# One core, convolution with generated kernels: quads in two halves, strips first and kernel pairs second, with two sets of PSUM banks

## What is computed

```
r = relu(bn(ln(x) @ w_reduce))                      # 32 channels
kgen = (r @ w_span + b_span) as (b, h, w, 16, 49)    # kernels, one for each pixel and group
x = x + sum over k of kgen[..., g, k] * patch(ln(x))[..., k, g, c]
t = tokens(x)                                        # 12544 x 128
probs = softmax(ln(t) @ gate_w + gate_b); the two largest are kept
t = t + sum over the two of prob_e * (gelu(ln(t) @ W1[e] + b1[e]) @ W2[e] + b2[e])
```

## Time and profile before

| | us |
|---|---|
| median of 3 runs | 1448.48 |
| lowest and highest | 1446.62 and 1455.89 |
| the profiled execution | 1449.3 |
| its span | 1447.5 |
| TensorE busy | 960.6 (66%) |
| ScalarE busy | 553.9 (38%) |
| VectorE busy | 497.3 (34%) |
| GpSimd busy | 488.6 (34%) |
| TensorE's granted clock, mean | 0.754 of full |

### The profile page before, as it was taken

The page is one execution under the profiler, slowest core; times in us unless marked ns, Lnnn a source line. Parts: engine busy times, 40 slices in busy tenths (PEclk is TensorE's granted clock), DMA queues, the critical chain, the costliest instruction groups (busy, mean ns, idle before and its releaser), DMA issues.

```text
span 1447.5 us, 29676 instructions
## 1 busy us (share of the span) xinstructions
PE 960.6 (66%) x11249; PEld 838.2 (58%) x11249; DVE 497.3 (34%) x1612; ACT 553.9 (38%) x1198; POOL 488.6 (34%) x536
## 2 busy tenths in 40 slices
PE   2687764888197792877928878379694687726540
PEld 1576653687096680876817768268583576725440
DVE  6111230345043450344513444123442235413432
ACT  5244330666054460453614545135351333312220
POOL 3000144012604517035171351712516136254425
PEclk9586665899598785897868778679876787656785
DMA  5659613463154532545425363252631422212322
GB/s 135 138 111 270 134 46 75 90 156 79 48 144 104 117 98 68 123 105 127 99 73 128 88 143 93 75 120 59 138 91 53 100 63 68 76 49 77 96 62 63
DMA packets 184078, 144.04 MB, mean 100 GB/s; under 512 B 65110, under 2 KB 169558, under 8 KB 183488
## 3 DMA queue, kind: packets, MB, share of 16 engines
q1 hardware_dynamic: 168114, 115.03, 33.2%
q0 software_dynamic: 14336, 25.72, 6.7%
q10 hardware_dynamic: 1486, 1.38, 0.4%
HBM read 89.70 MB, written 52.36 MB: 98 GB/s over the span
## 4 chain that ended last, share of the span: by engine, by line
PE 39%; issue 21%; another core or an unknown queue 10%; SPq 7%; ACT 7%; DVE 7%; POOL 3%; DVEq 2%; DMA 1%; ACTq 1%; POOLq 0%
PE e L1182 11%; PE kg L1148 9%; PE hy L1252 5%; PE hy L1262 5%; SPq L365 3%; POOL got L583 2%; PE back L1194 2%; ACT kb L662 2%; PE misc L1215 2%; DVEq L975 2%; ACT tn L677 2%; PE hy L1243 2%; SPq L431 1%; PE misc L1207 1%
## 5 line engine op out<-in xcount | busy, mean ns | idle before, releaser
L662 ACT ACTIVATE kb<-kg 112x896 f32<-112x896 f32 x224 | 205.6, 918 | 451.4 <-PE kg L1148 363.7
L1182 PE MATMUL e<-kb,win 112*32 112x64 f32 x6272 | 241.8, 291 | 182.3 <-issue 165.2
L583 POOL DMA_INDIRECT got<-yrows,pos x224 | 215.9, 964 | 331.9 <-DMA yrows<-yo 141.0
L1148 PE MATMUL kg<-rT,wk 98*112 98x112 f32 x1792 | 270.9, 313 | 75.5 <-ACT kb L662 42.2
L1182 PEld LDWEIGHTS e<-kb,win 112*32 112x32 f32 x6272 | 185.4, 131 | 230.1 <-issue 209.5
L569 POOL DMA_INDIRECT xrows<-tn,pos x224 | 213.8, 954 | 285.0 <-DVE pos L955 151.9
L1148 PEld LDWEIGHTS kg<-rT,wk 98*112 98x112 f32 x1792 | 233.9, 206 | 102.6 <-ACT kb L662 54.3
L712 ACT ACTIVATE hT<-hy,staged 128x128 f32<-128x128 f32 x490 | 152.6, 364 | 287.1 <-PE hy L1252 181.6
L1262 PE MATMUL hy<-staged,hT 128*128 128x128 f32 x980 | 179.7, 313 | 51.1 <-issue 22.3
L825 DVE TENSOR_TENSOR conv<-e,group_mask 128x448 f32<-128x448 f32 x112 | 69.7, 622 | 387.2 <-PE e L1182 258.4
L1252 PE MATMUL hy<-xT,staged 128*128 128x128 f32 x980 | 186.5, 321 | 19.1 <-issue 11.9
(11 more groups left out here) (113 smaller groups left out, 602.3 us busy)
## 6 DMA issues: line engine op xcount, KB each, us to landing
win<-xpad SPq DMA_DIRECT2D x56, 784.0 KB
xin<-xrows SPq DMA_DIRECT2D x56, 256.0 KB
yrows<-yo SPq DMA_DIRECT2D x56, 256.0 KB
t_row<-in_x_dram SPq DMA_DIRECT2D x64, 112.0 KB
xpad<-xs SPq DMA_DIRECT2D x240, 28.0 KB
out_dram<-t_row SPq DMA_DIRECT2D x56, 112.0 KB
xs<-in_x_dram SPq DMA_DIRECT2D x48, 112.0 KB
xrows<-tn SPq DMA_DIRECT2D x4, 896.0 KB, 14.6
```

Source lines behind the costliest of these rows:

```text
L583: pool.indirect_dma_start(got[:, slot * C:(slot + 1) * C], None, yrows[n % 2], bass.IndirectOffsetOnAxis(ap=pos[n % 2][:, k * COLS + c:k * ...
L662: act.activation(kb[:, lo:lo + 8 * PATCHES].rearrange("p (h k) -> p h k", h=2), kg[0:WIN, :].rearrange("p (h k) -> p h k", h=2)[:, :, 0:4 ...
L1148: mm = pe.matmul(kg_bank[j % 2][0:WIN, i * PATCHES:(i + 1) * PATCHES], wk[:, at:at + WIN], r[:, :, :, b4 + i], start=True, stop=True, skip ...
L1182: mm = pe.matmul(to, w[:, at:at + 32], rhs, start=True, stop=True, skip_group_check=True)
```

## The change

Each quad is split in two halves: the four strips in beats 0 to 7 (with the turns between them, the last at beat 8), and all eight pairs of the next quad in beats 8 to 15, one each. The visits move from even beats to odd ones, so that beats 15, 0 and 1 now have one each.

The eight PSUM banks are divided anew. There are two sets of two banks, `kg_set`. Strips alternate between the first bank of set 1 and the first bank of set 0 (`e_bank`), and `back` is the second bank of set 1. The pairs use set 0 and set 1 in turn (`set_of`), except for the pairs of the second quad of each chunk, which are made while `back` is still to be read: there only pairs 5 and 7 use set 1. A pair waits for the copy of the last pair in its own set (`pairs_out`), pair 0 for the last conv, and a pair in set 1 for the last `add_back`, which moves to beats 10 and 11 in the first quad of a chunk. A strip waits for the conv of the strip before the last. `kb` has four groups instead of six, so a copy waits until all strips of the quad before are done, and the special access pattern and turned mask for a ring that wraps go.

```diff
-    GSLOTS = 6
+    GSLOTS = 4
-    VISITS = (0, 1, 2, 4, 6, 8, 10, 12, 14)
+    VISITS = (0, 1, 3, 5, 7, 9, 11, 13, 15)
-        kg = ctx.enter_context(nc.psum_tensor("kg", [128, 1024], F32))
-        kg_bank = [kg[:, 0:512], kg[:, 512:1024]]
-        e_bank = bank("e")
+        kg_set = [ctx.enter_context(nc.psum_tensor(f"kg{i}", [128, 1024], F32)) for i in range(2)]
+        e_bank = [kg_set[1][:, 0:512], kg_set[0][:, 0:512]]
+        back = kg_set[1][:, 512:1024]
         misc = bank("misc")
-        back = bank("back")
+        def set_of(Q, p):
+            if Q == 0:
+                return p % 2
+            return int(p in ((5, 7) if Q % QUADS == 1 else (1, 3, 5, 7)))
+        def pairs_out(Q, p):
+            q0, p0 = divmod(8 * Q + p - 1, 8)
+            while q0 >= 0 and set_of(q0, p0) != set_of(Q, p):
+                q0, p0 = divmod(8 * q0 + p0 - 1, 8)
+            return 8 * q0 + p0 + 1
+        def strip_bank(t):
+            return e_bank[t % 2]
...
-                if g >= GSLOTS:
-                    act.wait_ge(main_done, 4 * ((g - GSLOTS) // 4 + 1))
+                if Q:
+                    act.wait_ge(main_done, STRIPS * Q)
...
-                if live and Q + 1 < QUADS * NC and j % 2:
-                    take_kernels(Q + 1, j // 2)
+                if live and Q + 1 < QUADS * NC and j >= 8:
+                    take_kernels(Q + 1, j - 8)
...
-                if live and j in ((12, 14) if o < 16 else (4, 8)):
-                    add_back(Q, int(j in (8, 14)))
+                if live and j in ((10, 11) if o < 16 else (4, 8)):
+                    add_back(Q, int(j in (8, 11)))
...
-                if j % 2 == 0 and pair:
-                    pe.wait_ge(kb_act, pair)
+                p = j // 2
+                if j % 2 == 0 and pairs_out(Q, p):
+                    pe.wait_ge(kb_act, pairs_out(Q, p))
+                if j == 0 and Q:
+                    pe.wait_ge(conv_ready, STRIPS * Q)
+                if j % 2 == 0 and Q and set_of(Q, p):
+                    pe.wait_ge(t_added, 2 * Q)
...
-                if t:
-                    pe.wait_ge(conv_ready, t)
+                if t >= 2:
+                    pe.wait_ge(conv_ready, t - 1)
...
-                    if more and j % 2:
-                        kernels(Q + 1, j - 1)
-                        kernels(Q + 1, j)
+                    if more and j >= 8:
+                        kernels(Q + 1, 2 * (j - 8))
+                        kernels(Q + 1, 2 * (j - 8) + 1)
```

More of the change, by code:

```diff
@@ L820, in take_conv @@
                 Q = t // STRIPS
-                turn = 2 if Q % 3 == 1 else 0
                 dve.wait_ge(main_done, t + 1)
@@ L825, in take_conv @@
                 nc.vector.tensor_tensor(conv[t % 2][:, :].rearrange("p (g k) -> p g k", g=4),
-                                        e_bank[:, 0:4 * T].rearrange("p (g k) -> p g k", g=4),
-                                        group_mask[:, turn:turn + 4].unsqueeze(2).to_broadcast([128, 4, T]),
+                                        strip_bank(t)[:, 0:4 * T].rearrange("p (g k) -> p g k", g=4),
+                                        group_mask[:, :].unsqueeze(2).to_broadcast([128, 4, T]),
                                         ALU.mult).then_inc(conv_ready, 1)
@@ L1147, in kernels @@
                     at = g * IMG + 57 - 8 * (b4 + i) - a
-                    mm = pe.matmul(kg_bank[j % 2][0:WIN, i * PATCHES:(i + 1) * PATCHES], wk[:, at:at + WIN],
+                    mm = pe.matmul(to[:, i * PATCHES:(i + 1) * PATCHES], wk[:, at:at + WIN],
                                    r[:, :, :, b4 + i], start=True, stop=True, skip_group_check=True)
@@ L1169, in apply @@
                 w = win[window_no(n, q // 2, s) % WSLOTS]
-                first = (4 * Q) % GSLOTS
                 for b in range(B):
                     p = (s // 2) * 56 + b * 14 + (s % 2) * 7 + pw
-                    if Q % 3 == 1:
-                        rhs = kb[:, :].rearrange("p (o g i k) -> p o g i k", o=3, g=2, i=POS)[:, 0:3:2, :, :, p]
-                        rhs = rhs.rearrange("p o g i -> p o (g i)")
-                    else:
-                        rhs = kb[:, first * POS * PATCHES:(first + 4) * POS * PATCHES]
-                        rhs = rhs.rearrange("p (i k) -> p i k", k=PATCHES)[:, :, p]
-                    to = e_bank[32 * b:32 * b + 32, 0:4 * T]
+                    rhs = kb[:, :].rearrange("p (i k) -> p i k", k=PATCHES)[:, :, p]
+                    to = strip_bank(t)[32 * b:32 * b + 32, 0:4 * T]
                     to = to.rearrange("p (g a w c) -> p g a w c", g=4, a=2, c=8)[:, :, :, pw, :]
```

8 lines of the change are left out of this document (4 added, 4 removed).

## The result

| | before | after |
|---|---|---|
| median, us | 1452.2 (4 runs, one more than above) | 1483.2 (4 runs, 1478.6 to 1491.6) |
| the profiled execution / its span | 1449.3 / 1447.5 | 1484.95 / 1483.2 |
| TensorE busy | 960.6 | 987.4 |
| TensorE's granted clock, mean | 0.754 | 0.754 |

The ratio of the times is 1.0233, with a 95% interval of 1.016 to 1.0306: the change made the kernel slower. The fourth run of the kernel before, 1471.5 us, was in a slower state and is left out of the ratio, though not of the median in the table.

The account below looks back on a forecast made before the run. TensorE was taken as gapless at full clock in visited stretches, but crawling in scatter windows, with copy round trips elsewhere. +6 us without visits and +16 for five visited chunks gave +22 on 1449.3: 1471 us, range 1436 to 1492.

Parts of the forecast that it names:

- quads 0 to 5: Quads without visits: first halves save nothing, serial pairs in quad 0 add 3.2 us; +6 us in sum, bounds 0 and +15.
- quads 6 and 7: The second chunk's visited half: -0.3 us in the second quad and +0.7 in the third, taken as nothing.
- five first quads: Router quad of each visited chunk: later scatters and strip 0 behind in the window, +1.8 us each, bounds -2.9 and +4.7.
- second quads: Second quad of visited chunks: copy latency gone (-0.7 us), back-to-back visits add 0.4; net -0.3 each.
- third quads: Third quad of visited chunks: ScalarE gets four copies more and one gelu less; +0.7 us each, between 0 and +1.5.
- fourth quads: VectorE's moments between close convs, more copies among ScalarE's LayerNorm pieces, partly taken in by stalls; +1.0 us each, bounds -2 and +4.
- rival C: Much slower: ScalarE bounds the second halves and serial pairs drop the clock each time; 1517 us, chance 0.07.
- the count of 184 instructions: Scatter window: TensorE executes a fixed 184 instructions, loads counted, so the new window holds 8 us of work, not 5.3.
- A: Faster: the waits for copies go and nothing takes their place; -34 us, 1415 us, chance 0.14.
- B: No change: the scatter window gives back all and the fourth quad is neutral; 1442 to 1453 us, chance 0.18.
- D: All is hidden: covers hold, the second set gives nothing, every term 0; 1449 us, chance 0.09.
- E: The scatters alone end the window, not a number of instructions, and nothing is given back; 1486 us, chance 0.07.

Follow-up runs that it names:

- the fill: Changed kernel plus unread matmuls in visited first quads: 12 ahead of ranks, 8 behind pair 0, 8 behind pair 2; ratio 1.0117 to the kernel before, 1473.7 us.
- the 15 chunks above: Visited chunks of three profiled executions: the changed kernel (median 1483.2 us), it once more (1494.4 us), and it with one strip bank (1482.8 us).
- plain transfers: GpSimd's 32 scatters a chunk made plain transfers to consecutive rows: kernel before 0.8175, 1188.7 us; changed kernel 0.8616, 1252.2 us.
- both sets in turn: Changed kernel with second-quad pairs also alternating between the two sets and add_back two beats earlier; ratio 1.0288 to the kernel before, 1500.7 us.
- a moved window: Changed kernel with positions and the tiles' experts at beat 13 instead of 9 and 10; ratio 1.0355 to the kernel before, 1512.8 us.

## Why the prediction was right, and where it was not

The forecast was 1471 us in a range of 1436 to 1492, slower with chance 0.50; the median is 1483.2. The sum was +22 on the profiled execution, which has +35.7. The direction was right, and so was the place of most of the loss; that the time lies inside the range owes something to luck, since the largest term came out at nearly three times its size and others came out smaller.

| term | forecast | measured |
|---|---|---|
| quads 0 to 5 | +6 | -0.5 |
| quads 6 and 7 | 0 | +5.8 |
| five first quads | +9 (1.8 each) | +24.6 (4.9 each) |
| second quads | -1.5 | -2.2 |
| third quads | +3.5 | +2.9 |
| fourth quads | +5 | +2.1 |
| behind the last conv | 0 | +2.9 |

**First quads.** The first step that was mis-sized is "scatters start about 0.7 us later than the 8.1 us after ranks". They start 4.1 us later on average. I had the waits right one by one (the cover gone, the turn waits for conv, ranks for cum, the round trip exposed; at the first scatter TensorE stands in visit 11) but priced them as time only. The rows at the lower level were at hand: pairs at 1.75 us behind serial waits. In rival C the clock drops at serial pairs, but not at ranks, and I gave it 0.07. Of the 4.1 us about 1.4 are the dependence (9.5 us at full clock for 8.1), which the prediction had at 0.7, and about 2.7 the clock, which it had at nothing. Two things show this: the fill, where the same chain with TensorE busy has its pairs at 1.02 us, and the chunks without fill in which the clock stayed up. The Trainium skill, "TensorE: Matmul & The Clock Gate", section A second HAM failure mode: psum-queue depth-cycling, describes frequent short idle times between groups of matmuls that make the clock oscillate. The trace agrees in part: waits of 0.50 and 1.49 us within 4 us, and the clock at 0.50 from 727.6 us on; but in two of the 15 chunks above it stayed at 0.97 and 1.00 with such waits.

**The window.** "8 us of work, not 5.3, and the serial waits of pairs cost nothing in it" was wrong, and with it the count of 184 instructions. From the entry into visit 11 to the last pair's signal at 784.17 the fourth window holds 112 instructions, loads counted, for 184 before, in the same 45 us. I had read TensorE's rows and not the signals: in a window these come up to 35 us behind the rows, and copies, gelus and convs wait for them. The forecast that strip 0 would enter the window later came true in three chunks of five, which lost 1.0 us on average for the 1.1 forecast (since the count is wrong, the agreement may be chance); in the other two strip 0 runs wholly behind the window, and they lost 4.1. On average the next conv came 2.3 us later after the first scatter. What gives back did exist, the 63 against 33 us with plain transfers. It gives back what is lost behind the first scatter and not what is lost ahead of it: over the five chunks the stretch from first scatter to next conv grew by 37.7 us with plain transfers and by 11.4 with scatters, that from ranks to first scatter by 15.8 and 20.4.

**Quads without visits.** The sum was +6 and is -0.5: quad 0 lost more than forecast, and a wait that has nothing to do with the pairs took it in. TensorE at quad 0 after the change:

```profile
77.64 1.02 PE L1169 MATMUL kg<-rT,wk 98*112 98x112 f32 x8 [1.01 <-ACT kb L679]
79.66 1.74 PE L1169 MATMUL kg<-rT,wk 98*112 98x112 f32 x8 [1.01 <-ACT kb L679]
82.41 1.75 PE L1169 MATMUL kg<-rT,wk 98*112 98x112 f32 x8 [1.01 <-ACT kb L679]
83.96 0.97 PE L1143 MATMUL misc<-ident,t_row 112*128 112x112 f32 x4
85.16 4.73 PE L1169 MATMUL kg<-rT,wk 98*112 98x112 f32 x24 [0.23 <-ACT kb L679]
```

The serial round trips came, at 2.02 and 2.75 us, and the clock stayed down for the three pairs behind them (4.73 us), though these wait for nothing: +7.2 for +3.2. Strips came 3.10 and 3.07 us apart, turns waiting 0.74 for conv, as worked out. Quads 1 and 2 are faster by 2.7 and 6.9 us and not slower by 0.3: in quad 1 the eight pairs take some 9.5 us at full clock, and a stall of 4.27 us in which a turn waited for conv at the end of quad 2 is gone (0.79 now). What held VectorE there, in the kernel before, is the statistics of the next image rows, which stand ahead of that conv and wait for their transfer:

```profile
144.40 1.64 DVE L781 BATCH_NORM_STATS2 st<-xs 112x6 f32<-112x128 f32 x8 [11.33 <-DMA xs<-in_x_dram]
```

After, they wait 7.24 us, until 141.94. In all 14 profiled executions they wait for this transfer and start between 141.6 and 145.5 us, whatever quad 0 took; with both sets in turn quad 0 is short and the turn waits 6.22 us instead. So the pairs' cost in quad 0 is real and is hidden by a transfer. I had counted stalls that could take in part of the cost in the fourth quad only.

**Quads 6 and 7** were called nothing, and cost 5.8. In the other runs with odd visits or halves quad 7 took 33.7 to 40.4 us, with the same edit 35.9 and 39.0: it varies from one execution to another by as much as the change. What makes it so is open.

**The signs.** "A wait of 2 us or more for cum" was 1.49 to 1.52 us in all five visited chunks: there, but shorter. The four chunks that can be taken from first conv to first conv last 186.6, 191.7, 191.3 and 187.1 us, two of them over the 190 beyond which I would have called ScalarE the bound. It is not: it is busy for 554 of 1483 us, in a window it starts behind TensorE's signal, and from the last conv of a fourth quad to the next quad's first (four chunks) it is busy for 18.3 to 19.0 us and TensorE for 24.5 to 29.1, so the sign "ScalarE busier than TensorE after beat 55" failed too.

**The rivals.** A (faster) had cum early by over 3 us; cum is late by 1.5. B (the window gives all back) and D (all is hidden) fell with the first quads; of the second set only the 7 us in TensorE's waits were left, with 10 us of new waits for `add_back` against them. E (nothing given back, 1486) has the nearest number, 3 us off the median. Its first half is borne out, the scatters alone end the window; its second is not: with plain transfers the loss doubles, so the window does give back. C (1517) had the right mechanism, the clock, at twice its size. The rule of the Trainium skill, "Runtime: NRT & Kernel Launch", Instruction fetch mechanics, by which streaming instructions costs next to nothing, is neither shown nor refuted here: the windows come with the indirect writes alone, but no run shows what in them holds TensorE up. The packets of 16 KB in the larger of the trace's two instruction queues are few in the windows (one or none between 5 us after the first scatter and 6 us after the last) and take no longer than outside (0.88 to 1.58 us everywhere); in the fourth window before, one lands at 737.7 us and the crawl goes on for 30 us.

**Settled and open.** Shown: by the ratios about 18 us come from moving the visits and about 15 from the rest of the change, taken as a whole (order in halves, banks, ring of four groups; only the second strip bank was taken out alone); the scatters start late by a dependence (1.4 us) and by the clock (0 to 3.2); in the windows ScalarE and VectorE wait for TensorE's signals. Argued only: that the 15 us lie wholly in the windows. Open: quad 7, the cost of a moved window, what delays the signals, and where the fill's other 12 us come from. No variant here beats the kernel before.

## What to carry to other kernels

When an edit takes work out from between two waits, price what the waits can do to TensorE's clock behind them, not their length alone: behind 1.5 us of waiting for cum and two round trips of 1.0 us the next 17 us ran at half clock, though not in every chunk. A quick test is a few matmuls that nothing reads in place of the wait. Where an engine crawls, read when its signals come beside its rows: an idle engine behind it may be waiting and not held up itself, and what you push into that stretch also delays all that waits for its signals. A second bank helps only where the order lets the engine run ahead into it. And a gain or loss ahead of a fixed transfer can vanish in the wait for it.

## What the runs showed of the hardware

- While GpSimd issues indirect writes back to back (32 at about 1.25 us each), TensorE crawls, and its signals reach the other engines up to 35 us behind the ends of its rows; ScalarE and VectorE start 0.02 us behind these signals. It ends 6.0 to 7.0 us after the last write's start. As many plain transfers from the same engine, issued in about 17 us for 39, do not do this, and the kernel before is 18% faster with them (1188.7 us).
- A window's cost depends on what it catches: moving it by 10 to 14 us cost 5 to 11 us each.
- Adding 28 matmuls to each visited first quad made the kernel 0.6 to 1.1% faster, by what it is set against, and 2.3% with plain transfers (1252.2 to 1223.8).
- TensorE stayed at the lower level for 17 us in which it was busy without a gap (17.00 of 17.00 us, clock 0.51).
- With the same wait of about 1.5 us for cum, the clock behind it was anything from 0.54 to 1.00 in 15 chunks.
